# P x V on 32 x 64 array tiles: the column halves take the two heads of a pair instead of two blocks of keys, and ScalarE alone empties the banks

## The chip, the cores and the metric

The kernel runs on one core of one Trainium2 chip. The metric is the device time of one execution in microseconds (us), lower is better. The engines are named as the profile names them: PE is TensorE's matmul side and PEld its weight load, DVE is VectorE, ACT is ScalarE, POOL is GpSimd, and SP issues the transfers.

## The reference

A "macaron" block on x of 2 sequences of 1024 tokens, width 1024, all in fp32: half a feed-forward layer, causal attention with low-rank queries and a shared low-rank latent for keys and values (32 heads, 16 pairs), and half the same feed-forward layer again. Cut to the attention's core:

```python
q = (rmsnorm(x @ wq_a.T) * w) @ wq_b.T            # 32 heads of 64 + 64 (rotary)
kv = rmsnorm(ckv) @ wkv_b.T                       # k_nope 64, v 128 per head, from one latent of 64
scores = einsum('bqhd,bkhd->bhqk', q_full, k_full) * softmax_scale
attn = softmax(where(causal, scores, min))
out = einsum('bqhk,bkhd->bqhd', attn, v).reshape(B, S, H * VD) @ wo.T
```

The kernel multiplies the probabilities by the 64-wide latent itself ("val"), since v is a linear function of it, and folds the value weights into wo.

## The kernel before

The program has phases: a feed-forward phase (f1), a phase for the latents, the attention phase, the output product that starts inside it, and a second feed-forward phase (f2). The change touches the attention phase alone.

**The steps.** Attention works through 32 steps: 16 pairs of heads, and for each pair the two sequences. A step's scores are 16 tiles: 8 rows of 128 queries (t) for each of the two heads (e); tile n is t = n // 2, e = n % 2, and because of causality its width is (t + 1) x 128 keys, at least 256 on TensorE. A prefix and shift name each job in the order tables at L895 to L903: "S8-1" is the job S for tile 8 of the step before.

- S (PE, `scores`): three fp32r products per piece into one of two 1024-wide score buffers in psS.
- M (DVE, L1408): adds the mask, takes the row maximum, and copies the tile to one of 8 `prob` buffers. The score buffer is free when M is done.
- E (ACT, L1357): the exponential in place, with the row sum.
- T (DVE, L1418): transposes each 32 x 32 block of a prob tile into pT. pT exists once; T for row t waits until P x V of the step before has read that row's part (`valued`).
- V (PE, `values`, L1294): P x V, below. V0 waits for T15 of its step.
- Q, F, W (PE): queries of the next step (six products of 512 columns each), the folded query weights (in every other step), and the folded output weights. They write the same four psV banks as V.
- ACT copies each Q out in three instructions (L626 to L628), and POOL rotates it (job A: L633, L635, L637); H (ACT, L644) and B (POOL, L648) split it into a high and a low part. S0 and S1 of a step wait for B0 and B1, S8 and S9 for B2 and B3.
- R (DVE, L1427, L1431) takes the reciprocal of the row sums; SP takes them through DRAM and back as `o_scale` (job X, L1206 and L1210), and P (POOL, L1481) multiplies the value tile `o_raw` by them; Y stores it (L1216).

Each engine runs its jobs strictly in the order of its own table; the tables are written out by hand or by a planner, and the waits are semaphores. In one turn of TensorE's table come S8 to S15 of the step before with Q, F and W among them, then S0 to S7 of this step, then V0 to V7 of the step before.

**P x V.** DVE transposes only within 32 x 32 blocks, so a row group of the array (32 rows) holds 32 keys of four different query blocks i, and each row group i writes its own psV bank i. For each key tile kt (V0 to V7) there are four blocks of 32 keys. Each product has 32 rows and 64 stationary columns (val of one block), and moves both heads at once: 2 x (8 - kt) x 32 columns. Blocks 0 and 1 go to output partitions 0 to 63, blocks 2 and 3 to partitions 64 to 127: 16 products for a key tile. In the trace each of them is two loads and two matmuls. So each bank holds two halves of a sum, which have to be added: ACT copies the upper half (64 x 512) to the unused upper rows of cosT or sinT (`evict_values`, L1366 to L1372; `upper`, L1171), and DVE adds it to the lower half in two instructions, one for each head (`join_values`, L1433 to L1443), and writes o_raw. The profile calls o_raw, o_scale and the query buffers "pT", since they lie in its unused columns.

**The end.** In the last turn DVE splits the first 8 output weights before its four joins, and the other 8 after them; the output product (`tensor_steps`, L1088 in the trace) runs its first pairs meanwhile.

Of the kernel before, what the change touches and what calls it, by code (L numbers as in the profile page):

```python
# [8 lines left out]
ALU = mybir.AluOpType  # L9
ACT = mybir.ActivationFunctionType  # L10
# [6 lines left out]
P = 128  # L17
BANK = 512
# [5 lines left out]
PAIRS = H // 2  # L24
NOPE, ROPE, VD = 64, 64, 128
QHD = NOPE + ROPE
KVR = 64
# [7 lines left out]
QT = S // P  # L35
# [52 lines left out]
def later(n, least):  # L88

    return not isinstance(n, int) or n >= least  # L90
# [104 lines left out]
SLOTS = 4  # L195
# [455 lines left out]
def latents_phase(nc, k, src_d, args, ahead, v_d):  # L651
# [6 lines left out]
    with ExitStack() as stack:  # L658
# [179 lines left out]
        def _(dve):  # L838
# [53 lines left out]
TILES = 2 * QT  # L892
RING = 8
BLOCKS = P // 32
PE_STEP = ("S8-1 F0-1 S9-1 F1-1 Q0+0 S10-1 S11-1 Q1+0 S12-1 S13-1 W0-1 S14-1 S15-1 Q2+0 Q3+0 S0+0 S1+0 S2+0 S3+0 S4+0 "  # L895
           "S5+0 S6+0 S7+0 V0-1 V1-1 V2-1 V3-1 V4-1 V5-1 V6-1 V7-1")
ACT_STEP = ("F0-1 F1-1 E8-1 Q0+0 E9-1 E10-1 Q1+0 E11-1 W0-1 H0+0 E12-1 E13-1 H1+0 E14-1 E15-1 Q2+0 Q3+0 E0+0 E1+0 E2+0 "
            "E3+0 E4+0 E5+0 E6+0 H2+0 E7+0 H3+0 O0-1 O1-1 O2-1 O3-1")
DVE_STEP = ("M15-1 T12-1 T13-1 M0+0 T14-1 M1+0 M2+0 M3+0 T15-1 M4+0 M5+0 T0+0 R1-1 T1+0 T2+0 M6+0 T3+0 M7+0 T4+0 T5+0 "
            "T6+0 R0+0 T7+0 O0-1 M8+0 O1-1 F0+0 M9+0 O2-1 T8+0 F1+0 M10+0 M11+0 T9+0 O3-1 M12+0 M13+0 T10+0 T11+0 "  # L900
            "M14+0")
POOL_STEP = ("B2+0 B3+0 A0+1 A1+1 B0+1 B1+1 P0-1 P1-1 A2+1 A3+1")
SP_STEP = ("X1-1 Y0-1 Y1-1 K0+0 L0+0 X0+0 Z0+0")  # L903


# [201 lines left out]
def attention_phase(nc, k, args, oT_d, rinv_d, wvo_d, v_d, src_d, dst_d):  # L1107
# [6 lines left out]
    with ExitStack() as stack:  # L1114
        c = Ctx(nc, stack)
        queries, cosT, sinT, wn_in, tab_in = k.queries, k.cosT, k.sinT, k.wn_in, k.tab_in
# [6 lines left out]
        pT = c.sb("pT", [P, 2, QT, S])  # L1123
        val = c.sb("val", [P, B, BLOCKS, QT, KVR])
# [5 lines left out]
        psV = c.ps("psV", [P, 4, BANK])  # L1130
# [1 line left out]
        scored, maxed, allowed, exped, turned = c.sem("scored"), c.sem("maxed"), c.sem("allowed"), c.sem("exped"), c.sem("p_turned")  # L1132
        zeroed, recip, r_turned = c.sem("zeroed"), c.sem("recip"), c.sem("r_turned")
        r_stored, r_loaded = c.sem("r_stored"), [c.sem(f"r_loaded{ch}") for ch in range(2)]
        valued, copied, evicted, scaled = c.sem("valued"), c.sem("copied"), c.sem("evicted"), c.sem("scaled")
        o_stored = [c.sem(f"o_stored{ch}") for ch in range(2)]
        w_done, w_copied, w_stored = c.sem("w_done"), c.sem("w_copied"), c.sem("w_stored")
        output = Output(nc, c, {**k.homes, **c.homes}, psS, src_d, dst_d, oT_d, wvo_d, k.early, k.eps_ln)
        units = 2 * PAIRS
        block = stack.enter_context(nc.Block())  # L1140

        def spare(e, t0, t1):

            return pT[:, e, t0:t1, CHUNK:S]

        qf, swapped = spare(0, 0, 2), spare(0, 2, 4)
        o_raw, o_scale = spare(1, 0, 2), spare(1, 2, 4)
# [19 lines left out]
        def folds(it, n, s):  # L1167

            return 2 * (it + (s + 1) // 2) + n + 1

        def upper(bank):  # L1171

            return (cosT, sinT)[bank // 2][0:KVR, bank % 2 * BANK:(bank % 2 + 1) * BANK]

        def by_block(tile, i):

            return tile.rearrange("p h (t a r) -> p h t a r", a=BLOCKS, r=32)[:, :, :, i, :]
# [81 lines left out]
        def _(pe):  # L1259
# [34 lines left out]
            def values(it, kt, s):  # L1294

                step, b = it * 2 + s, s % 2
                if kt == 0:
                    pe.wait_ge(turned, step * TILES + TILES)
                    if not later(step, 2):
                        pe.wait_ge(v_in[step], 16 * BLOCKS * BLOCKS)  # L1300
                for a in range(BLOCKS // 2):
                    for half in range(2):
                        for i in range(BLOCKS):
                            rows, block = slice(32 * i, 32 * i + 32), BLOCKS // 2 * half + a
                            x = kt * P + 32 * block
                            out = psV[KVR * half:KVR * half + KVR, i, :].rearrange("p (e t r) -> p e t r", e=2, r=32)
                            ins = nc.tensor.matmul(out[:, :, kt:QT, :], val[rows, b, block, kt, :], pT[rows, :, kt:QT, x:x + 32],  # L1307
                                                   start=(kt == 0 and a == 0), stop=(kt == QT - 1 and a == BLOCKS // 2 - 1))
                ins.then_inc(valued, 1)

            def fold_output(it, s):
# [8 lines left out]
            def body(r):  # L1320
                for (job, n, s), users in r.bank_users(PE_STEP):
                    vacated(r.it, users)
# [17 lines left out]
        def _(act):  # L1340
# [25 lines left out]
            def evict_values(it, bank, s):  # L1366

                step = it * 2 + s
                act.wait_ge(valued, step * QT + QT)
                if later(step, 1):  # L1370
                    act.wait_ge(evicted, step * 4 + bank - 3)
                nc.scalar.activation(upper(bank), psV[KVR:P, bank, :], ACT.Copy).then_inc(copied, 1)  # L1372

            def body(r):
                for job, n, s in r.jobs(ACT_STEP):
                    if job == "E":
# [24 lines left out]
        def _(dve):  # L1401
# [28 lines left out]
                    dve.wait_ge(r_stored, number * 64 - 192)  # L1430
                nc.vector.transpose(rinvT[:, x // QT, :], rinv[:]).then_inc(r_turned, 1)  # L1431

            def join_values(it, bank, s):  # L1433

                step = it * 2 + s
                dve.wait_ge(copied, step * 4 + bank + 1)
                if later(step, 1):
                    for ch in range(2):
                        dve.wait_ge(o_stored[ch], step * 16)
                for e in range(2):  # L1440
                    x = slice(e * 32 * QT, (e + 1) * 32 * QT)
                    halves = [y.rearrange("p (h t r) -> p h t r", h=2, r=32) for y in (psV[0:KVR, bank, x], upper(bank)[:, x])]
                    ins = nc.vector.tensor_tensor(by_block(o_raw, bank)[KVR * e:KVR * e + KVR], halves[0], halves[1], ALU.add)  # L1443
                ins.then_inc(evicted, 1)

            nc.vector.memset(rinv[:], 1.0).then_inc(zeroed, 1)
            dve.wait_ge(zeroed, 1)

            def body(r):
                for job, n, s in r.jobs(DVE_STEP):  # L1450
                    if job == "M":
                        maxima(r.it, n, s)
                    elif job == "T":
                        transposes(r.it, n, s)
                    elif job == "R":
                        row_scales(r.it, n, s)
                    elif job == "O":
                        if r.last and s == 1 and n == 0:
                            output.weights_lo(nc, dve, range(2 * SLOTS))
                        join_values(r.it, n, s)  # L1460
                    elif job == "F":
                        queries.split_fold_lo(nc, dve, psV[:, n, :], n, folds(r.it, n, s))
            rounds(dve, body)
            output.weights_lo(nc, dve, range(2 * SLOTS, PAIRS))
            output.vector_steps(nc, dve)

        @block.gpsimd
        def _(pool):
# [20 lines left out]
            def body(r):  # L1489
                job, n, s = list(Round(0).jobs(POOL_STEP))[-1]  # L1490
                before = None if r.first else (job, n, s - 2)
                for job, n, s in r.jobs(POOL_STEP):
                    if before:
# [122 lines left out]
```

## Time and profile before

| | |
|---|---|
| time, median of 3 runs | 1892.49 us (1891.0 to 1895.84) |
| span of the profiled execution | 1895.1 us |
| granted TensorE clock, mean over the span | 0.985 |
| DMA | 182.7 MB, 96 GB/s |
| attention steps | 32, one every 29.55 us and 30.96 us in turn |

The profile is of one execution and was taken on the core itself. Its views used below: the page's shares and 40 slices (a digit is the busy share of a slice in tenths); busy time by stretches; the waits, which say for an engine and a line which other line ended its idle time; groups of instructions by line and form with the mean duration of one; and the timeline, in which equal neighbours are merged ("x256") and the time covers all of them. A matmul's duration holds the way through the array, so that durations of neighbours overlap: the pace is read from starts.

### The profile page before, as it was taken

Reading aid. Unit: us, or ns where it says so; the run is one execution under the profiler, and the core shown is the slowest. Engines: PE = TensorE matmul, PEld = TensorE weight load, DVE = VectorE, ACT = ScalarE, POOL = GpSimd, SP = SyncE. Lnnn points to the kernel's source line nnn. Section 1 sums busy time; section 2 is a strip of 40 time slices with the busy share of each in tenths; the row PEclk is TensorE's granted clock in tenths of the full one; section 3 lists DMA queues with packets and bytes.
Section 4 is the critical chain, followed back from the end, with each engine's and each line's share of the span. In section 5 each row is a group of like instructions: output and inputs, shape, how many; then the busy total and the mean of one; then the engine's idle time right before and its main releaser. Section 6 shows DMA issues by size and latency. Waiting matters only on the chain. (4 is left out here: it accounts for less than half of the span.)

```text
span 1895.1 us, 44298 instructions
## 1 busy us (share of the span) xinstructions
PE 1803.7 (95%) x15472; PEld 1422.9 (75%) x15472; DVE 1231.4 (65%) x2654; ACT 1000.5 (53%) x2137; POOL 877.8 (46%) x641
## 2 busy tenths in 40 slices
PE   5999969899999999999999999998999999989999
PEld 4788869877777777777777777775788888877887
DVE  5655358688898888889888888989521111125453
ACT  2221047788887888888787888877310100112110
POOL 3232112377777878777787878775000000014321
PEclk9999979999999999999999999999999999989999
DMA  6542162311212112121222212123742233224321
GB/s 217 193 156 100 67 173 94 84 62 44 86 59 78 57 62 80 57 80 40 85 69 68 69 51 82 55 86 113 249 151 89 94 100 115 67 87 158 130 89 59
DMA packets 111969, 182.74 MB, mean 96 GB/s; under 512 B 27680, under 2 KB 64672, under 8 KB 109856
## 3 DMA queue, kind: packets, MB, share of 16 engines
q1 hardware_dynamic: 111904, 181.88, 29.8%
q8 instruction: 41, 0.67, 0.2%
q14 instruction: 24, 0.20, 0.0%
HBM read 122.33 MB, written 59.51 MB: 96 GB/s over the span
## 5 line engine op out<-in xcount | busy, mean ns | idle before, releaser
L1290 PE MATMUL psS<-keyT,q 128*128 128x512 f32 (+2 forms) x2304 | 473.2, 350 | 23.9 <-POOL q L648 14.5
L1290 PEld LDWEIGHTS psS<-keyT,q 128*128 128x128 f32 x2304 | 381.2, 189 | 118.2 <-DVE negmax L1408 41.7
L1357 ACT ACTIVATE prob<-prob,negmax 128x640 f32<-128x640 f32 (+7 forms) x512 | 392.0, 767 | 78.5 <-DVE negmax L1408 75.9
L1418 DVE STREAM_TRANSPOSE pT<-prob 128x640 f32<-128x640 f32 (+7 forms) x512 | 379.9, 762 | 66.4 <-PE psV L1307 61.6
L1408 DVE CUSTOM_DVE_ANT_0 prob<-psS,mask 128x640 f32<-128x640 f32 (+7 forms) x512 | 371.9, 742 | 20.9 <-PE psS L1290 7.4
L469 PE MATMUL f_psy<-f_weff,f_xT 128*128 128x512 f32 x1344 | 315.6, 393 | 0.0
L1101 PE MATMUL psS<-o_w,o_o 128*128 128x512 f32 x1344 | 304.8, 389 | 0.0
L469 PEld LDWEIGHTS f_psy<-f_weff,f_xT 128*128 128x128 f32 x1344 | 250.9, 188 | 55.8
L1101 PEld LDWEIGHTS psS<-o_w,o_o 128*128 128x128 f32 x1344 | 252.3, 188 | 52.4
L1307 PE MATMUL psV<-pT,val 32*64 32x512 f32 (+3 forms) x8192 | 264.8, 407 | 6.4 <-DVE pT L1418 6.2
L1307 PEld LDWEIGHTS psV<-pT,val 32*64 32x64 f32 x8192 | 168.8, 132 | 109.7 <-issue 66.2
L633 POOL TENSOR_TENSOR pT<-pT,cosT 64x512 f32<-64x512 f32 x124 | 159.6, 1287 | 194.4 <-ACT pT L628 180.5
L275 POOL TENSOR_TENSOR f_weff<-f_w_in,f_weff 128x1024 fp32r<-128x1024 f32 x16 | 39.0, 2437 | 397.5 <-ACT f_weff L388 397.5
L618 PE MATMUL psV<-qnT,wq 128*128 128x512 f32 x744 | 186.4, 393 | 0.4 <-issue 0.4
L1074 DVE TENSOR_TENSOR o_y<-psS,o_x_in 128x512 f32<-128x512 f32 x32 | 22.0, 691 | 252.0 <-PE psS L1101 238.4
L351 POOL TENSOR_TENSOR f_xo<-f_xt,f_bias_half 128x1024 f32<-128x1024 f32 x32 | 81.4, 2543 | 216.7 <-DMA x<-f_xo 103.5
L1023 ACT ACTIVATE o_o<-o_in 128x1024 fp32r<-128x1024 f32 x32 | 32.6, 1055 | 257.2 <-PE psS L1101 235.8
L648 POOL TENSOR_TENSOR q<-pT,q 128x512 fp32r<-128x512 f32 x124 | 160.1, 1291 | 10.9 <-POOL pT L637 2.2
L635 POOL TENSOR_TENSOR pT<-pT,sinT 64x512 f32<-64x512 f32 x124 | 160.0, 1290 | 9.7
L637 POOL TENSOR_TENSOR pT<-pT 64x512 f32<-64x512 f32 x124 | 159.5, 1286 | 9.7
L618 PEld LDWEIGHTS psV<-qnT,wq 128*128 128x128 f32 x744 | 135.3, 188 | 27.0 <-issue 0.6
L179 ACT ACTIVATE f_xT<-f_ps_xT 128x512 fp32r<-128x512 f32 x64 | 35.0, 595 | 172.6 <-PE f_ps_xT L170 172.6
(120 smaller groups left out, 1919.1 us busy)
## 6 DMA issues: line engine op xcount, KB each, us to landing
wo<-in_wo SPq DMA_DIRECT2D x16, 1024.0 KB, 6.0
pT<-row_scales SPq DMA_DIRECT2D x128, 128.0 KB, 2.9
oT<-pT SPq DMA_DIRECT2D x64, 256.0 KB, 2.5
o_in<-oT SPq DMA_DIRECT2D x32, 512.0 KB, 5.2
f_xt<-in_x SPq DMA_DIRECT2D x16, 512.0 KB, 4.4
f_w_in<-in_w SPq DMA_DIRECT2D x16, 512.0 KB, 6.7
w_sum<-f_w_in SPq DMA_DIRECT2D x16, 512.0 KB, 5.3
x<-f_xo SPq DMA_DIRECT2D x16, 512.0 KB, 3.0
```

Source lines behind the costliest of these rows:

```text
L469: ins = nc.tensor.matmul(psy[:, j, half, :], f.xT[:, j, a, dt, :], weff[:, b, m, dt, half * BANK:(half + 1) * BANK], start=(i == 0 and dt ...
L618: ins = nc.tensor.matmul(bank, self.wq[:, a, e, t, :], qnT[:, m, t, x:x + CHUNK], start=(i == 0 and t == 0), stop=(i == 2 and t == QRT - 1))
L633: nc.gpsimd.tensor_tensor(plain, plain, cos, ALU.mult).then_inc(self.rope_parts, 1)
L635: nc.gpsimd.tensor_tensor(crossed, crossed, sin, ALU.mult).then_inc(self.rope_parts, 1)
L637: nc.gpsimd.tensor_tensor(plain, plain, crossed, ALU.add).then_inc(self.roped, 1)
L648: nc.gpsimd.tensor_tensor(self.rows(LO, n), qf, self.rows(HI, n).bitcast(F32), ALU.subtract).then_inc(self.q_lo, 1)
L1101: ins = nc.tensor.matmul(self.ps[:, j, x], self.o[j][:, a, pair, :], self.w[pair][:, m, x], start=(pair == 0 and i == 0), stop=(pair == PA ...
L1290: ins = nc.tensor.matmul(psS[:, slot, start + x0:start + x1], q[:, e, a, t * P:(t + 1) * P], k.keyT[:, m, b * S + x0:b * S + x1], start=(i ...
L1307: ins = nc.tensor.matmul(out[:, :, kt:QT, :], val[rows, b, block, kt, :], pT[rows, :, kt:QT, x:x + 32], start=(kt == 0 and a == 0), stop=( ...
L1357: nc.scalar.activation(row, row, ACT.Exp, bias=negmax[:, n % 8:n % 8 + 1], scale=-1.0, accum_out=rowsum[:, column(n, s):column(n, s) + 1]) ...
L1408: nc.vector.tensor_tensor_reduce(out=prob[:, n % RING, 0:width], in0=place(n), in1=k.mask[:, S - width:S], scale=-1.0, scalar=LARGEST, op0 ...
L1418: nc.vector.transpose(pT[:, n % 2, t, 0:width], prob[:, n % RING, 0:width]).then_inc(turned, 1)
```

## The change

In `values`, a product now takes one head e and one block of 32 keys. The head decides which 64-column half of the array and which 64 output partitions it uses; the four blocks of a key tile accumulate in the same place. So there are 32 products for a key tile instead of 16, each moving (8 - kt) x 32 columns instead of twice that, and val of a block is loaded once for each head. A finished bank holds 128 partitions (two heads x 64) by 256 columns of complete sums. ACT copies it to o_raw in one instruction of 128 x 256 (`evict_values`), and waits itself for the store of the step before to be done with o_raw. The joins on DVE, the semaphore `copied` and the helper `upper` are gone. In the last turn DVE splits all 16 output weights after its table.

The order tables of PE, ACT, DVE and POOL are new, SP's is not. PE: F1 ahead of S9, and W behind S14. ACT: the copy of bank 3 (O3) moves into the next turn, behind F0; W behind H0; E14 ahead of H1; Q2 ahead of E15. DVE: M and T in another order, without joins, R1 directly behind T15, T0 and T1 ahead of M4 and M5. POOL: the two scalings P0 and P1 move from behind B1 to directly behind B3, ahead of A0.

```diff
-PE_STEP = ("S8-1 F0-1 S9-1 F1-1 Q0+0 S10-1 S11-1 Q1+0 S12-1 S13-1 W0-1 S14-1 S15-1 Q2+0 Q3+0 S0+0 S1+0 S2+0 S3+0 S4+0 "
+PE_STEP = ("S8-1 F0-1 F1-1 S9-1 Q0+0 S10-1 S11-1 Q1+0 S12-1 S13-1 S14-1 W0-1 S15-1 Q2+0 Q3+0 S0+0 S1+0 S2+0 S3+0 S4+0 "
            "S5+0 S6+0 S7+0 V0-1 V1-1 V2-1 V3-1 V4-1 V5-1 V6-1 V7-1")
-ACT_STEP = ("F0-1 F1-1 E8-1 Q0+0 E9-1 E10-1 Q1+0 E11-1 W0-1 H0+0 E12-1 E13-1 H1+0 E14-1 E15-1 Q2+0 Q3+0 E0+0 E1+0 E2+0 "
-            "E3+0 E4+0 E5+0 E6+0 H2+0 E7+0 H3+0 O0-1 O1-1 O2-1 O3-1")
-DVE_STEP = ("M15-1 T12-1 T13-1 M0+0 T14-1 M1+0 M2+0 M3+0 T15-1 M4+0 M5+0 T0+0 R1-1 T1+0 T2+0 M6+0 T3+0 M7+0 T4+0 T5+0 "
-            "T6+0 R0+0 T7+0 O0-1 M8+0 O1-1 F0+0 M9+0 O2-1 T8+0 F1+0 M10+0 M11+0 T9+0 O3-1 M12+0 M13+0 T10+0 T11+0 "
-            "M14+0")
-POOL_STEP = ("B2+0 B3+0 A0+1 A1+1 B0+1 B1+1 P0-1 P1-1 A2+1 A3+1")
+ACT_STEP = ("F0-1 O3-2 F1-1 E8-1 Q0+0 E9-1 E10-1 Q1+0 E11-1 E12-1 E13-1 H0+0 W0-1 E14-1 H1+0 Q2+0 E15-1 Q3+0 H2+0 E0+0 "
+            "E1+0 E2+0 E3+0 E4+0 E5+0 E6+0 E7+0 H3+0 O0-1 O1-1 O2-1")
+DVE_STEP = ("T12-1 T13-1 M15-1 T14-1 M0+0 M1+0 M2+0 M3+0 T15-1 R1-1 T0+0 T1+0 M4+0 M5+0 T2+0 M6+0 M7+0 T3+0 T4+0 T5+0 "
+            "T6+0 M8+0 F0+0 R0+0 T7+0 M9+0 F1+0 T8+0 M10+0 M11+0 T9+0 T10+0 M12+0 M13+0 T11+0 M14+0")
+POOL_STEP = ("B2+0 B3+0 P0-1 P1-1 A0+1 A1+1 B0+1 B1+1 A2+1 A3+1")
...
-                for a in range(BLOCKS // 2):
-                    for half in range(2):
+                for block in range(BLOCKS):
+                    for e in range(2):
                         for i in range(BLOCKS):
-                            rows, block = slice(32 * i, 32 * i + 32), BLOCKS // 2 * half + a
-                            x = kt * P + 32 * block
-                            out = psV[KVR * half:KVR * half + KVR, i, :].rearrange("p (e t r) -> p e t r", e=2, r=32)
-                            ins = nc.tensor.matmul(out[:, :, kt:QT, :], val[rows, b, block, kt, :], pT[rows, :, kt:QT, x:x + 32],
-                                                   start=(kt == 0 and a == 0), stop=(kt == QT - 1 and a == BLOCKS // 2 - 1))
+                            rows, x = slice(32 * i, 32 * i + 32), kt * P + 32 * block
+                            out = of_block(psV[KVR * e:KVR * e + KVR, i, :])
+                            ins = nc.tensor.matmul(out[:, kt:QT, :], val[rows, b, block, kt, :], pT[rows, e, kt:QT, x:x + 32],
+                                                   start=(kt == 0 and block == 0), stop=(kt == QT - 1 and block == BLOCKS - 1))
...
                 if later(step, 1):
-                    act.wait_ge(evicted, step * 4 + bank - 3)
-                nc.scalar.activation(upper(bank), psV[KVR:P, bank, :], ACT.Copy).then_inc(copied, 1)
+                    for ch in range(2):
+                        act.wait_ge(o_stored[ch], step * 16)
+                nc.scalar.activation(by_block(o_raw, bank), of_block(psV[:, bank, :]).rearrange("p (h t) r -> p h t r", h=2),
+                                     ACT.Copy).then_inc(evicted, 1)
...
-                for e in range(2):
-                    x = slice(e * 32 * QT, (e + 1) * 32 * QT)
-                    halves = [y.rearrange("p (h t r) -> p h t r", h=2, r=32) for y in (psV[0:KVR, bank, x], upper(bank)[:, x])]
-                    ins = nc.vector.tensor_tensor(by_block(o_raw, bank)[KVR * e:KVR * e + KVR], halves[0], halves[1], ALU.add)
-                ins.then_inc(evicted, 1)
...
-                        if r.last and s == 1 and n == 0:
-                            output.weights_lo(nc, dve, range(2 * SLOTS))
-                        join_values(r.it, n, s)
...
-            output.weights_lo(nc, dve, range(2 * SLOTS, PAIRS))
+            output.weights_lo(nc, dve, range(PAIRS))
```

`of_block(bank)` is the first 256 columns of a bank, seen as 8 rows t of 32.

## Rows read from the trace of the kernel before

**Rows 1.** The page: busy us, share of the span and instructions by engine

```profile
PE 1803.7 (95%) x15472; PEld 1422.9 (75%) x15472; DVE 1231.4 (65%) x2654; ACT 1000.5 (53%) x2137; POOL 877.8 (46%) x641
```

**Rows 2.** Busy us by stretches, from one V start to the next; then clock

```profile
871.09:902.04 30.95, 30.17 (x366) 22.60 (x365) 26.88 (x65) 25.44 (x58) 23.34 (x19) 1.00 0.16 54
902.04:931.59 29.55, 28.78 (x357) 21.52 (x356) 25.94 (x61) 24.65 (x55) 23.05 (x19) 1.00 0.23 80
```

**Rows 3.** Waits of PE and PEld, 500 to 1250 us: total, times, longest

```profile
PE psS L1290 <- POOL q L648: 12.3, 37, 0.4
...
PEld psS L1290 <- DVE negmax L1408: 29.5, 49, 0.8
PEld psS L1290 <- POOL q L648: 13.2, 37, 0.6
...
PEld psV L1307 <- DVE pT L1418: 9.1, 25, 0.4
```

**Rows 4.** Timeline of one V: start, us covered, instructions; then its end alone

```profile
902.04 8.21 PE L1307 MATMUL psV<-pT,val 32*64 32x512 f32 x256
...
909.41 0.84 PE L1307 MATMUL psV<-pT,val 32*64 32x128 f32 x48
...
909.30 0.81 PEld L1307 LDWEIGHTS psV<-pT,val 32*64 32x64 f32 x48
```

**Rows 5.** L1307 alone by key tile, kt = 0, 5, 6 and 7: stretch, us

```profile
902.03:903.80 1.77, 1.76 (x32) 0.77 (x40) 1.00 0.74 168
...
908.53:909.18 0.65, 0.65 (x40) 0.64 (x32) 1.00 0.00 0
909.18:909.63 0.46, 0.46 (x48) 0.46 (x36) 1.00 0.00 0
909.63:910.20 0.56, 0.56 (x48) 0.47 (x34) 1.00 0.02 7
```

**Rows 6.** Groups by form, whole span: busy us, mean ns; idle before

```profile
L1307 PEld LDWEIGHTS psV<-pT,val 32*64 32x64 f32 x8192 | 168.8, 132 | 109.7 <-issue 66.2 <-DVE pT L1418 10.2 <-ACT pT L628 0.6
...
L1443 DVE TENSOR_TENSOR pT<-psV,cosT 64x256 f32<-64x256 f32 x128 | 53.2, 416 | 26.4 <-ACT cosT L1372 25.5
...
L1372 ACT ACTIVATE cosT<-psV 64x512 f32<-64x512 f32 x64 | 34.6, 590 | 19.4 <-PE psV L1307 19.4
...
L777 ACT ACTIVATE qnT<-ps 128x256 fp32r<-128x256 f32 x16 | 6.1, 382 | 1.4 <-PE ps L821 1.4
```

**Rows 7.** Timeline from the end of that V to the next V

```profile
910.64 1.12 PE L1290 MATMUL psS<-keyT,q 128*128 128x384 f32 x6 [0.39 <-POOL q L648]
...
913.94 1.17 SPq L1210 DMA_DIRECT2D pT<-row_scales  x2
...
914.63 0.60 ACT L626 ACTIVATE pT<-psV 128x512 f32<-128x512 f32 x1 [0.78 <-PE psV L618]
...
924.86 2.69 POOL L648 TENSOR_TENSOR q<-pT,q 128x512 fp32r<-128x512 f32 x2
...
926.48 1.14 ACT L1357 ACTIVATE prob<-prob,negmax 128x1024 f32<-128x1024 f32 x1
...
926.97 4.70 PE L1290 MATMUL psS<-keyT,q 128*128 128x256 f32 x24
...
927.81 2.67 POOL L1481 TENSOR_TENSOR pT<-pT 128x512 f32<-128x512 f32 x2 [0.26 <-POOL q L648]
...
930.03 1.24 DVE L1418 STREAM_TRANSPOSE pT<-prob 128x1024 f32<-128x1024 f32 x1
...
931.59 8.21 PE L1307 MATMUL psV<-pT,val 32*64 32x512 f32 x256
```

**Rows 8.** Timeline behind the last V: ACT's copies, DVE's joins, PE's wait

```profile
1339.41 1.08 ACT L1372 ACTIVATE cosT<-psV 64x512 f32<-64x512 f32 x2
...
1342.31 1.73 DVE L1443 TENSOR_TENSOR pT<-psV,sinT 64x256 f32<-64x256 f32 x4
...
1347.64 35.52 PE L1088 MATMUL psS<-o_w,o_o 128*128 128x512 f32 x144 [4.35 <-DVE o_w L1054]
```

More of the change, by code:

```diff
@@ L1134, in attention_phase @@
         r_stored, r_loaded = c.sem("r_stored"), [c.sem(f"r_loaded{ch}") for ch in range(2)]
-        valued, copied, evicted, scaled = c.sem("valued"), c.sem("copied"), c.sem("evicted"), c.sem("scaled")
+        valued, evicted, scaled = c.sem("valued"), c.sem("evicted"), c.sem("scaled")
         o_stored = [c.sem(f"o_stored{ch}") for ch in range(2)]
@@ L1169, in folds, with of_block @@
             return 2 * (it + (s + 1) // 2) + n + 1
-        def upper(bank):
-            return (cosT, sinT)[bank // 2][0:KVR, bank % 2 * BANK:(bank % 2 + 1) * BANK]
+        def of_block(bank):
+            return bank[:, 0:32 * QT].rearrange("p (t r) -> p t r", r=32)
         def by_block(tile, i):
@@ L1431, in row_scales @@
                 nc.vector.transpose(rinvT[:, x // QT, :], rinv[:]).then_inc(r_turned, 1)
[L1433 to L1439, printed above, removed]
-                for e in range(2):
-                    x = slice(e * 32 * QT, (e + 1) * 32 * QT)
-                    halves = [y.rearrange("p (h t r) -> p h t r", h=2, r=32) for y in (psV[0:KVR, bank, x], upper(bank)[:, x])]
-                    ins = nc.vector.tensor_tensor(by_block(o_raw, bank)[KVR * e:KVR * e + KVR], halves[0], halves[1], ALU.add)
-                ins.then_inc(evicted, 1)
             nc.vector.memset(rinv[:], 1.0).then_inc(zeroed, 1)
@@ L1456, in body @@
                         row_scales(r.it, n, s)
-                    elif job == "O":
-                        if r.last and s == 1 and n == 0:
-                            output.weights_lo(nc, dve, range(2 * SLOTS))
-                        join_values(r.it, n, s)
                     elif job == "F":
```

## The prediction

> **What bounds the kernel now.** I read the busy shares first, then the stretches between V starts, then the waits, then the timeline. PE is busy for 95% of the span and DVE for 65% [rows 1], so over the whole program only PE can be the bound. In attention that is less clear: in a step of 29.55 us PE is busy for 28.78, DVE for 25.94, ACT for 24.65 and POOL for 23.05 [rows 2]. The reader is to see four engines that are all nearly full and run fixed orders: a step is a loop of waits rather than one busy engine. PE's waits from 500 to 1250 us (25 steps) are small: DVE's maxima 29.5 us, POOL's split queries 13.2 and 12.3 (largely the same stalls, seen by the load and the matmul), the last transpose before V 9.1 [rows 3], some 2 us a step. So the change can win back 2 us of PE's time a step at most, and all else that it gives DVE is worth nothing.
>
> I cut a step in two: **V itself**, 8.21 us, and **the way from V's end to the next V's start**. One V runs from 902.04 to 910.25 and the next starts at 931.59 [rows 4, 7], so the way is 21.34 us; in a step with the two folds it is 30.95 - 8.21 = 22.74 [rows 2].
>
> **V: twice as many products, each half as long.** The moved columns stay the same, so where a product is bound by its columns nothing changes: two products of 256 for one of 512. It changes where the columns are so few that the instruction is the bound. The key tiles take 1.77 us (kt 0), 0.65 (kt 5), 0.46 (kt 6) and, with what is left of 8.21, about 0.4 (kt 7) [rows 5]. Per matmul of 32 that is 55, 20, 14 and 13 ns, for 512, 192, 128 and 64 columns: it falls with the columns down to 128 and then no longer. The floor, from V's end: 48 matmuls cover 0.84 us, less the last one's own 0.25, over 47 steps: 12.6 ns; 48 loads cover 0.81, less 0.13: 14.5 ns [rows 4]. I take 13.5 ns. After, a key tile has 64 matmuls and never takes under 64 x 13.5 = 0.86 us. Kt 4 (128 columns then) is at it already. Added: kt 5 0.86 - 0.65 = 0.21, kt 6 0.86 - 0.46 = 0.40, kt 7 0.86 - 0.40 = 0.46, and some 0.05 of seams in the other five: **+1.1 us a step**. Low end: 12.6 ns, +0.9. High end: a load takes 132 ns [rows 6], and if eight are under way at a time and no more, 16.5 ns each, 1.06 us a key tile: kt 4 +0.19, kt 5 +0.41, kt 6 +0.60, kt 7 +0.66, +1.9 us a step. The trace has short products only at V's end, behind a full queue; whether the pace holds for 256 of them it doesn't show. I stay near the rows measured back to back.
>
> The trace thus shows 13 ns for a matmul of 64 columns [rows 4]. The Trainium skill, TensorEngine Tiling, section Performance Considerations (Instruction Overhead), speaks against this change: each matmul has some 60 cycles of overhead, and one should not tile a dimension that is already small. Taken as 25 ns an instruction at 2.4 GHz, an estimate from that page, V would last at least 512 x 25 ns = 12.8 us instead of the 9.3 that the rows give. By that rule 256 instructions now would need 6.4 us, which 8.21 allows, but its last 48 would need 1.2 us and take 0.84, so the trace disagrees.
>
> **V's end to the next V.** *ACT.* Four copies of 64 x 512 at 590 ns become four of 128 x 256, for which a row of the same size reads 382 ns [rows 6]; the new output pattern is not in the trace, so 0.38 to 0.6. The new waits on `o_stored` cost nothing while the outputs are stored 20 us before. Behind the copies stands E8, and behind that the copy of Q0, which needs PE's S8, S9 and Q0 anyway: S8 takes 1.12 us for 6 matmuls now with its neighbour gap, clean about 0.87. Clean, S8 and S9 end at 1.74 us after V and Q0 at 3.1, and ACT's Q0 copy starts at 3.4; even at 0.6 each the copies end at 2.4 and E8 (0.93) at 3.3. *DVE.* Eight additions of 416 ns go [rows 6], 3.3 us a step, and with them M8 to M13 are no longer queued behind the joins. *PE.* S8 waited 0.39 us for POOL [rows 7] and S9 again; POOL gets P (2.67 us for two, now between B1 and A2 [rows 7]) out of the way, and Q2 is copied before E15, so B2 and B3 are ready by V's end. Now the Q0 copy starts at 914.63, 4.38 after V's end; after at 3.4.
>
> From there the loop goes through ACT's queue. From the Q0 copy to E15 (914.63 to 926.48) ACT does Q0, E9, E10, Q1, E11, W, H0, E12, E13, H1, E14 in 11.85 us, of which about 0.45 is waiting [rows 7]; the new order has the same set up to H1, so H1 ends at 3.4 + 11.4 = 14.8, with 0.1 to 0.3 for new waits 15.0. Then POOL's B1, 1.3 us, ends at 16.4 and S1 starts at 16.6; now B1 ends at 924.86 + 2.69 = 927.55, which is 17.3. S1 to S7 need 3.45 clean (PE's 927.3 to 931.4 is 4.1 with DVE's stalls). The next V starts at 20.0 instead of 21.34. T15 is next latest: H1 15.0, Q2 1.8, E15 1.15, T15 1.24 [rows 7] and 0.3 to V make 19.5, so it is hidden with 0.5 to spare. In fold steps the order adds 1.25 (two folds 1.1 and their ACT copies) instead of 1.4. **Won back: 1.3 and 1.5, 1.4 us a step.** Bounds: nothing, if one of the moved jobs comes late; 2.0 if PE ran free.
>
> *POOL and SP.* P now stands ahead of A0, which must start at 5.2 (Q0 copied). P needs all four copies (1.9 after V, 2.9 in a fold step) and its scales. Those loads are issued at 913.94 now, 3.7 after V's end [rows 7], and would be late there: P would end at 10.4. But they sit there because SP first had to issue the stores of a P that ran at 927.81. With P early SP is free; its K waits for W's copy at 13.4, the first scale job follows with the 8 us it takes now, the second starts at about 22 and has landed by 29, just at V's end (20.0 + 9.3). R1, now straight after T15, is ready long before. So P runs 2 to 5 us after V, and A0 is not held; the margin is 2 us.
>
> **The end.** Behind the last V DVE's joins end at 1344.0 and PE waits 4.35 us, to 1347.6, for the ninth output weight [rows 8]. Without joins DVE starts 1.7 us earlier, ACT's copies are 0.4 shorter: PE goes on at about 1345.5, **-2.1**, and the last V's own growth is hidden by this wait.
>
> **Sum.** 31 x (1.1 - 1.4) = -9.3, end -2.1: -11.4 on the profiled 1895.1 gives 1883.7; the median lies 2.6 below the profiled span, so **1881 us**. The term that carries it is a difference of two like numbers, each uncertain by half a microsecond a step, or 15 us.
>
> **The rivals.**
> - *Slower: the short products run at 16.5 ns.* Place: kt 4 to 7 of every V. Price: +1.9 for +1.1, 31 x 0.8 = +25: 1906. It decides the sign from 13.5 + 1.5 ns on (0.36 us a step over some 224 matmuls). For it: loads alone come in stretches of 14.5 ns; against: the 12.6 of matmuls. Chance 0.25. Beyond it, the same mechanism with kt 5's 20 ns as the least that a long train of short products keeps: kt 3 to 7 then take 1.28 us each, +3.0 a step for +1.1, +59: 1940, chance 0.02. The Trainium skill's rule above points this way; with its 25 ns it would be 3.5 us a step and 1989, an estimate from that page.
> - *Slower: P holds A0.* If scales or copies land late, every us moves A0, A1, B0, B1, S1 and V; it eats the gain from 1.4 on. With P at 7.5 instead of 5.2: +2.3 in the 16 steps that have K, +37, or half of that: 1900 to 1918. Chance 0.13.
> - *Faster: PE runs free.* If B1 is no limit (H1 earlier than I queue it), V follows at 19.3: 0.7 x 31 = -22: 1859. Chance 0.15.
> - *It doesn't do what it says*: the copies cost 0.6 or more. Hidden by Q0, as above; no time of its own.
>
> Forecast 0.42, own range 1871 to 1894; the rest 0.03. The range 1859 to 1912 leaves out 0.2. Faster means below 1886.8, slower above 1898.2, since 0.3% is about what a measurement can tell from none. Forecast case: 0.30 faster, 0.11 same, 0.01 slower; free PE 0.14 faster, 0.01 same; short products 0.05 same, 0.22 slower; P late 0.02 faster, 0.03 same, 0.08 slower; the rest slower. Together 0.46, 0.20, 0.34.
>
> **What would show it.** V: 9.3 us from start to end, kt 5 to 7 each about 0.86. The way: S8 within 0.2 us of V's end; Q0's copy at 3.4; S1 at 16.6 behind POOL's B1, V at 20.0. Periods 29.3 and 30.5. P at 2 to 5 after V. Wrong: V over 9.7 (the pace), A0 behind P, or DVE's maxima still among PE's waits.

## The result: 13% slower, and the profile after

The changed kernel takes **2150.49 us** (median of 4, 2139.67 to 2153.14) where the kernel before takes 1893.61 (median of 4, 1891.0 to 1895.84) in the same comparison: a ratio of **1.1345**, 95% interval 1.1316 to 1.1375. The forecast was 1881 with a range of 1859 to 1912. The profiled execution spans 2150.4 us, 255 more than before's.

The busy shares come first, as in [rows 1], and two more lines of the page below them: the granted clock in 40 slices, and one DMA queue.

```profile
PE 1909.2 (89%) x23664; PEld 1595.6 (74%) x23664; DVE 1149.9 (53%) x2398; ACT 976.7 (45%) x2137; POOL 875.1 (41%) x641
...
PEclk9999899989989899889888989989889999999999
...
q8 instruction: 209, 3.42, 0.7%
```

DVE has lost its 256 joins (82 us), ACT 24 us, and PE has 8192 more matmuls, as the diff says. PE's busy share *fell*, from 95% to 89%: it stands still for longer. The clock is at 8 tenths in many slices where before's was at 9 in nearly all. And the queue q8, which carries instructions and was 41 packets and 0.67 MB before, carries 209 packets and 3.42 MB. The page of before, for comparison:

```profile
PEclk9999979999999999999999999999999999989999
...
q8 instruction: 41, 0.67, 0.2%
```

What PE waits for over the whole span (line, releaser, us in total, times, longest):

```profile
PE psV L1305 <- issue: 109.1, 78, 4.2
PE psS L1289 <- issue: 57.7, 13, 4.7
```

"Issue" means that no semaphore, engine or transfer that the profile knows holds the engine back. In attention before, PE's matmuls have two such waits, of 0.4 and 0.2 us; there they wait as in [rows 3], and the 12.3 us for POOL is no longer among PE's longer waits. L1305 is the product P x V, L1289 the score product, of which the first behind a V is meant.

One V in the timeline, to be laid beside [rows 4] (start, us covered, instructions, in brackets the idle time before):

```profile
811.12 3.81 PE L1305 MATMUL psV<-pT,val 32*64 32x256 f32 x142
815.44 2.64 PE L1305 MATMUL psV<-pT,val 32*64 32x192 f32 x128 [0.51 <-issue]
819.19 1.95 PE L1305 MATMUL psV<-pT,val 32*64 32x128 f32 x128 [1.11 <-issue]
822.93 1.50 PE L1305 MATMUL psV<-pT,val 32*64 32x64 f32 x114 [1.79 <-issue]
```

The pieces behind the first are 128 matmuls long, with as many loads, whatever the columns. A key tile has 64 matmuls, so two of them are as long; but the first stop comes after 142 matmuls (14 into the third key tile), and in the next V after 284 (28 into the fifth). So it is neither a key tile's data nor a bank that PE waits for. And in this V, the shorter the products, the longer the stop. The next V ends like this; the loop's back branch stands behind it:

```profile
857.19 1.35 PE L1305 MATMUL psV<-pT,val 32*64 32x64 f32 x100 [2.11 <-issue]
862.74 1.97 PE L1289 MATMUL psS<-keyT,q 128*128 128x384 f32 x6 [4.20 <-issue]
```

Stretches over one turn of PE's loop (two steps), with the columns of [rows 2]: V, the first scores, the rest of the way, then V again and the whole way behind it.

```profile
811.12:824.45 13.33, 9.92 (x514) 8.86 (x513) 5.27 (x16) 5.73 (x18) 7.19 (x6) 0.99 0.19 64
824.45:829.30 4.85, 4.85 (x20) 4.55 (x21) 2.61 (x8) 2.14 (x6) 2.58 (x2) 0.68 0.14 54
...
846.08:858.54 12.46, 9.62 (x513) 8.83 (x512) 5.06 (x16) 5.73 (x18) 7.21 (x6) 0.99 0.08 27
858.54:888.86 30.32, 25.36 (x109) 20.50 (x108) 19.14 (x41) 19.04 (x39) 16.02 (x13) 0.78 0.16 56
```

V takes 13.3 and 12.5 us for 8.21, of which PE is busy for under 10, and behind it the granted clock is 0.68 and 0.78. The DMA view of the same turn counts, beside the data on q1, this:

```profile
q8 instruction: 12, 0.20, 1.1%
```

Twelve blocks of 16 KB (0.20 MB) are fetched in one turn. In a turn of before (811.12 to 871.09) the same view has q1 alone. The stops in V lie 256 PE instructions apart (or a multiple of it), and 16 KB over 256 is 64 bytes an instruction: the stops lie at the seams of the fetched blocks. The transfers fit too. In the whole trace after, V has 70 stops of over 0.5 us; 69 of them end 2.2 to 3.0 us after the start of a transfer on q8, and the last one is a wait for DVE's transpose.

**The account.** From the first V's start to the last one's end the kernel before takes 945 us, the changed one 1208: all of the loss, and 8 us more. Idle times of over 0.65 us between PE's matmuls sum to 7 us in before (2 of them) and 170 in after (85): +162. The clock is at its lower level, 1.2 GHz, for 7 us there before and for 234 after; in the turn shown it falls at V's end, behind stops of 0.5, 1.1 and 1.8 us and again behind 0.7 and 2.1. PE is busy for 176 of the 234 us. The first six score products behind a V take 1.97 us at the lower level and, in e2 below, half of 2.05 at the upper one, so about half of the 176 is lost, 88 us (an estimate). In the turn shown, 77.7 us for 60.5 in [rows 2], the stops of V and of the back branch sum to 10.5 (0.5, 1.1, 1.8, then 0.7, 2.1 and 4.2) and another behind them is 0.6. The clock takes 1.6 behind the first V (4.85 x 0.32) and 4.3 behind the second (half of the 8.6 us that PE is busy at 0.50). That is 17.0 for a loss of 17.2. What the short products add and what the order gives are not in it; by the runs below they nearly cancel out.

### The profile page after: what moved, and what is told of

Same layout as the page of the kernel before. It is cut to its first block and busy times, and to the rows that moved or that the text cites. A ratio compares the mean times of both kernels' runs of the same rounds, so it can differ in the third digit from the quotient of the medians.

```text
span 2150.4 us, 60219 instructions
## 1 busy us (share of the span) xinstructions
PE 1909.2 (89%) x23664; PEld 1595.6 (74%) x23664; DVE 1149.9 (53%) x2398; ACT 976.7 (45%) x2137; POOL 875.1 (41%) x641
## 3 DMA queue, kind: packets, MB, share of 16 engines
q8 instruction: 209, 3.42, 0.7%
## 5 line engine op out<-in xcount | busy, mean ns | idle before, releaser
L1408 DVE CUSTOM_DVE_ANT_0 prob<-psS,mask 128x640 f32<-128x640 f32 (+7 forms) x512 | 377.6, 749 | 362.6 <-PE psS L1289 344.8
L1289 PE MATMUL psS<-keyT,q 128*128 128x512 f32 (+2 forms) x2304 | 502.5, 371 | 65.7 <-issue 57.7
L1289 PEld LDWEIGHTS psS<-keyT,q 128*128 128x128 f32 x2304 | 415.2, 208 | 150.5 <-issue 86.9
L1305 PE MATMUL psV<-pT,val 32*64 32x256 f32 (+2 forms) x16384 | 316.9, 297 | 113.9 <-issue 109.1
L1305 PEld LDWEIGHTS psV<-pT,val 32*64 32x64 f32 x16384 | 285.9, 134 | 153.0 <-issue 132.0
L1464 POOL TENSOR_TENSOR pT<-pT 128x512 f32<-128x512 f32 x64 | 82.2, 1285 | 350.2 <-ACT pT L1371 340.2
L618 PE MATMUL psV<-qnT,wq 128*128 128x512 f32 x744 | 204.8, 421 | 2.2 <-issue 2.2
L618 PEld LDWEIGHTS psV<-qnT,wq 128*128 128x128 f32 x744 | 149.2, 208 | 32.8 <-issue 2.9
```

The lines of the kernel that those rows point to most:

```text
L618: ins = nc.tensor.matmul(bank, self.wq[:, a, e, t, :], qnT[:, m, t, x:x + CHUNK], start=(i == 0 and t == 0), stop=(i == 2 and t == QRT - 1))
L1289: ins = nc.tensor.matmul(psS[:, slot, start + x0:start + x1], q[:, e, a, t * P:(t + 1) * P], k.keyT[:, m, b * S + x0:b * S + x1], start=(i ...
L1305: ins = nc.tensor.matmul(out[:, kt:QT, :], val[rows, b, block, kt, :], pT[rows, e, kt:QT, x:x + 32], start=(kt == 0 and block == 0), stop= ...
L1408: nc.vector.tensor_tensor_reduce(out=prob[:, n % RING, 0:width], in0=place(n), in1=k.mask[:, S - width:S], scale=-1.0, scalar=LARGEST, op0 ...
```

## The experiments

My theory after the profile: **PE's loop body no longer stays where PE reads its instructions from, so it is fetched anew in each turn, and in V, where the instructions are shortest, PE is through a block before the next has arrived.** The rivals: the array's halves taken by heads, or the new order, cost the time by themselves (e1, e2); it is short products at V's end, not their number (e3, e4); it is not the number of instructions but the kind of product (e11 with e10 as its control, e13). All edits are in P x V, in the tables, or in the passes.

**Every product split, everything else as before (e1).** Banks, joins and tables are those of before; each product runs once per head.

```diff
-                    for half in range(2):
+                    for heads in (slice(0, 1), slice(1, 2)):
+                      for half in range(2):
...
-  nc.tensor.matmul(out[:, :, kt:QT, :], val[rows, b, block, kt, :], pT[rows, :, kt:QT, x:x + 32],
+  nc.tensor.matmul(out[:, heads, kt:QT, :], val[rows, b, block, kt, :], pT[rows, heads, kt:QT, x:x + 32],
```

> The kernel before with one thing changed: in all eight key tiles each product is split by head, so there are as many PE instructions as after the change (16384 matmuls of P x V) while the tables, the joins on DVE and the layout of the sums stay. Fetch theory (PE's loop body no longer stays in its instruction store, so it is fetched again every turn and P x V runs out of instructions): the instruction queue moves some 3.4 MB instead of 0.67, the stretch of one V is 12 to 14 us with gaps of 1 to 2.5 us every second key tile, and the time is 2120 to 2170 us. Rival, the new order tables or ACT's wait for o_stored: they are not in this kernel, so it stays at the pace of short products alone, 1893 + 32 x 1.1 = 1928 us, with 0.67 MB of instructions.

2215.31 us, ratio 1.1688 (1.1666 to 1.1709): more than the changed kernel and more than expected. Of the 65 us between the two, e2 below gives 36 to the joins and the order that e1 keeps. On its page, the instruction queue:

```profile
q8 instruction: 209, 3.42, 0.7%
```

And PE's waits, whole span:

```profile
PE psV L1308 <- issue: 145.8, 88, 4.5
PE psS L1290 <- issue: 55.9, 13, 4.5
```

The number of products alone brings the loss, twelve fetches a turn with it. The heads' place in the array, the tables and ACT's wait for `o_stored` are cleared. Another 29 us between e1 and the changed kernel are not explained; e1's V is longer, 12 to 17 us.

**The new order without the split (e2).** The changed kernel with before's 16 products a key tile. The joins are left out and ACT's copies take the first 256 columns of a bank, so the two halves are never added: less is computed.

```diff
-                for block in range(BLOCKS):
-                    for e in range(2):
+                for a in range(BLOCKS // 2):
+                    for half in range(2):
...
```

> The kernel after with one thing taken back: P x V issues before's 16 products a key tile (both heads in each, the column halves take different blocks). The halves of the sums are not added and ACT copies only the first 256 columns of a bank, so the joins are left out of the computation; copies, waits, tables and DVE's relief are those of after. Fetch theory: 0.67 MB of instructions, V back at 8.2 us, and the order change can show its worth: my prediction's 1.4 us a step and 2.1 at the end give 1893 - 45 = 1848 us. Rival (tables or waits are what costs): still over 2100 us.

1857.6 us, ratio 0.9805 (0.9789 to 0.9822). Its q8 is back at before's 41 packets. The timeline from one V to the next, beside [rows 7]:

```profile
887.07 8.21 PE L1306 MATMUL psV<-pT,val 32*64 32x512 f32 x256
...
895.21 2.05 PE L1289 MATMUL psS<-keyT,q 128*128 128x384 f32 x12
895.31 1.21 ACT L1372 ACTIVATE pT<-psV 128x256 f32<-128x256 f32 x4 [1.54 <-PE psV L1306]
...
896.69 2.67 POOL L1465 TENSOR_TENSOR pT<-pT 128x512 f32<-128x512 f32 x2 [1.51 <-ACT pT L1372]
...
898.73 0.60 ACT L626 ACTIVATE pT<-psV 128x512 f32<-128x512 f32 x1 [0.27 <-PE psV L618]
...
908.94 2.69 POOL L648 TENSOR_TENSOR q<-pT,q 128x512 fp32r<-128x512 f32 x2
...
915.48 6.83 PE L1306 MATMUL psV<-pT,val 32*64 32x512 f32 x163
```

V ends at 895.28. S8 runs straight on, the Q0 copy starts 3.45 us after V's end, POOL's B1 ends 16.35 after it, and the next V starts at 20.20: the way that the prediction worked out (3.4, 16.4, 20.0). So the order gives what it should where nothing is fetched, and without the split there is no loss: the level of 1.2 GHz, too, is granted for 3.4 us in its attention and not for 234.

**The split in a part of the key tiles (e3, e4, e7, e9).** As e1, but only for the key tiles named.

```diff
+  for heads in ([slice(0, 1), slice(1, 2)] if kt in (0, 1, 2) else [slice(0, 2)]):   # e3
+  for heads in ([slice(0, 1), slice(1, 2)] if kt in (5, 6, 7) else [slice(0, 2)]):   # e4
+  for heads in ([slice(0, 1), slice(1, 2)] if kt in (7,) else [slice(0, 2)]):        # e7
+  for heads in ([slice(0, 1), slice(1, 2)] if kt in (6, 7) else [slice(0, 2)]):      # e9
```

> The kernel before with the products of key tiles 0 to 2 alone split by head: 192 more PE instructions in a step, 384 in the loop body (about 1500 to 1890, of 64 bytes: 94 to 118 KB). The columns are 256, 224 and 192 there, so that the stream is the bound. If the instruction store holds 128 KB: no more fetches than before, V at 8.25 us and 1893 to 1897 us. If it holds less than 118 KB: fetches in every turn, and 50 to 150 us more.

> The kernel before with the products of key tiles 5 to 7 alone split by head (96, 64 and 32 columns): the same number of added instructions as e3 (118 KB), but all of them short. It prices short products without the others. My prediction's 13.5 ns each: key tiles at 0.86 us, +1.1 us a step, 1893 + 34 = 1927 us or less where the slack of the step takes some. Rival (short products alone run dry, at 25 ns or more each): +3 us a step and more, above 1975 us.

> The kernel before with key tile 7 alone split by head: 64 more PE instructions in a step, 128 in the loop body (about 1630, 102 KB). Looks for the limit between 94 KB (no fetches) and 118 KB (nine in every turn). If it lies above 102 KB: 0.67 MB, key tile 7 longer by 0.3 to 0.45 us, 1894 + 12 = 1906 us. If below: seven or eight fetches in every turn, over 2.2 MB, and 150 us or more on top.

> The kernel before with key tiles 6 and 7 split by head: a loop body of about 1760 PE instructions, 112 to 113 KB, between e7 (102 KB, none fetched) and e3 (118 KB, nine in every turn). If the limit is in whole blocks of 16 KB and seven of them fit (112 KB), this one lies on it; with fetches: eight or nine a turn, 2.4 MB or more and over 2020 us; without: 0.67 to 0.7 MB and 1900 to 1910 us.

| kernel | matmuls in the body | q8 packets | fetches a turn | us | ratio (95%) |
|---|---|---|---|---|---|
| before | 720 | 41 | 0 | 1893.6 | 1 |
| e7, kt 7 | 784 | 42 | 0 | 1899.74 | 1.0027 (1.0011 to 1.0042) |
| e9, kt 6, 7 | 848 | 98 | 2 and 7 in turn | 1997.98 | 1.0547 (1.0526 to 1.0568) |
| e3, kt 0 to 2 | 912 | 162 | 9 | 2084.57 | 1.1014 (1.0990 to 1.1039) |
| e4, kt 5 to 7 | 912 | 162 | 9 | 2113.78 | 1.1158 (1.1109 to 1.1206) |
| e1, all | 1232 | 209 | 12 | 2215.31 | 1.1688 (1.1666 to 1.1709) |

e3 splits only the longest products, which stay at 192 columns or more (before's key tile 5 has as many in one product) and so were free by every price that the prediction worked out from rows. It costs 10%. e4 was made to price the short products and can't, being fetched as e3 is. The first 64 matmuls more cost 6 us, the next 64 cost 98. That is a step between two sizes of the body and not a price for each product. (For e9 I had expected eight or nine fetches in every turn and over 2020 us.) e3's waits are of after's two kinds:

```profile
PE psV L1308 <- issue: 61.1, 33, 3.6
PE psS L1290 <- issue: 50.3, 13, 4.6
```

**Many instructions with V untouched (e13).** Before, with the three passes of the score and query products issued twice (the sums come out doubled). V's 16 products a key tile stay.

```diff
-                    for i, (a, m) in enumerate(PASSES):
+                    for i, (a, m) in enumerate(PASSES * 2):
```

> The kernel before with each pass of the scores' and the queries' fp32r products issued twice (they are then summed double, so the scores are twice too large): the loop body has 912 matmuls, as many as e3, of which 384 are fp32r and 528 belong to fp32 products as in before. If all PE instructions count alike: nine fetches a turn as in e3, 2.6 MB. If an fp32 product takes more room than an fp32r product beyond its two matmuls (e7 and e11 say so), none: 0.6 to 0.75 MB, V at 8.2 us. PE's own work grows by some 17 us a step either way, so the time is about 2350 to 2450 us.

2538.46 us, above the 2350 to 2450 that I had put on it; most of the growth is the second set of passes. It has 912 matmuls in the body, like e3, and exactly e3's 162 packets, nine a turn. Its V and what follows it:

```profile
1019.56 8.21 PE L1307 MATMUL psV<-pT,val 32*64 32x512 f32 x256
1032.17 3.07 PE L1290 MATMUL psS<-keyT,q 128*128 128x384 f32 x12 [4.40 <-issue]
```

Here V is whole again, at 8.21 us, though the body is fetched: its block of 16 KB lasts longer, and the fetches keep up. The stop at the back branch stays (61.4 us over 13 times). So there are two costs: the back branch, whatever the body holds, and the stops in stretches of short instructions. The odd steps, with the back branch, take 54 to 58 us; the first of them, which is not yet fetched, takes 47.9. That is 6 to 10.5 us a turn, of which 4 to 5 are the stop; the rest fits the clock behind it, which is at its lower level for 3 to 14 us a turn.

**Fewer instructions elsewhere to make room (e10, e11).** Scores and queries with one pass of three (two products are left out), first alone (e10), then with key tiles 0 to 2 split (e11).

```diff
-                    for i, (a, m) in enumerate(PASSES):
+                    for i, (a, m) in enumerate(PASSES[:1]):
```

> The control for e11: the kernel before with one of the three passes of the scores' and the queries' products (the two correction passes are left out), a body of some 1250 PE instructions. No fetches, V at 8.2 us; the steps end up with DVE or ACT as the bound, some 26 to 28 us.

> e3 with the same two correction passes left out as in e10: the split of key tiles 0 to 2 is there in full, but the body has some 1630 PE instructions instead of 1890, as many as e7's. Fetch theory: no fetches, V back from e3's 10 and 13 us to 8.2 to 8.3, time within 0.3% of e10's. Rival (the split products cost by themselves, as weight loads or banks): V stays at 10 us and more, and the time is 60 us or more above e10's.

e10: 1929.11 us, ratio 1.0183 (1.0163 to 1.0204). With less work for PE it is slower: PE waits for the other engines and its mean granted clock falls to 0.87 of 2.4 GHz, from 0.985. Its V takes 9.6 to 11.1 us though nothing is fetched there, so V's length says nothing in e11, and the packets have to decide. e11: 1979.31, ratio 1.0448 (1.0427 to 1.0469), 50 us over e10. I had expected it to be free of fetches, at 784 matmuls in the body like e7. It fetches two and seven blocks in turn, like e9. This is a miss, and it limits the theory: between e7 and e11 the number of matmuls does not decide. Both lie at the edge; where the body stands against the 16 KB blocks may, which I did not vary.

**V with few instructions but short ones (e6).** The changed kernel, with key tiles 1 to 4 reduced to one product each (their part of the result is left out), to see the pace of split products that are not fetched.

```diff
+                            if kt in (1, 2, 3, 4) and (block, e, i) != (3, 1, 3):
+                                continue
```

> The kernel after with most of P x V's key tiles 1 to 4 left out (one product of 32 each instead of 32), so that its body has as many instructions as before's (about 1520) and still holds the short products of key tiles 5 to 7. Fetch theory: 0.67 MB of instructions, no gaps, key tiles 5 to 7 at 0.80 to 0.86 us each (13 ns a matmul), whole time under 1820 us. Rival (short products starve PE by themselves): key tiles 5 to 7 at 1.6 us or more, gaps of a microsecond as in after.

1827.99 us in one run (I had expected under 1820), 41 packets, no stops in V. V without the four key tiles:

```profile
869.97 5.20 PE L1307 MATMUL psV<-pT,val 32*64 32x256 f32 x264
```

From first start to last, key tile 7 takes 0.65 us for 64 matmuls; key tile 6 takes 0.68 to 0.84 from its start to the next one's. Key tile 5 takes 1.09 to 1.16, here right behind the single products; in the changed kernel, where no stop falls into it, 0.80 to 0.84.

**What in the order earns it (e5, e12).** e2 with all of before's tables (e5), and e2 with only POOL's place of P as before (e12, whose edit against e2 stands below).

```diff
-POOL_STEP = ("B2+0 B3+0 P0-1 P1-1 A0+1 A1+1 B0+1 B1+1 A2+1 A3+1")
+POOL_STEP = ("B2+0 B3+0 A0+1 A1+1 B0+1 B1+1 P0-1 P1-1 A2+1 A3+1")
```

> e2 with before's order tables (without the joins in DVE's): the computation leaves out the joins as e2 does. It splits e2's 36 us. If they come from the empty places of the joins in DVE's queue (my prediction: DVE's maxima no longer late), most of it stays: 1858 to 1870. If the new order brings it (P ahead of A0, O3 and W later, R1 earlier), it falls back to 1880 to 1893.

> e2 (wide products, joins left out, after's tables) with before's order on POOL alone: P0 and P1 behind B1 again. My prediction said P ahead of A0 makes room so that B2 and B3 are ready at V's end. If that carries the order's 25 us (e2 against e5): 1875 to 1883. If ACT's order (Q2 ahead of E15, copies first) carries it: 1857 to 1865.

e5: 1882.85, ratio 0.9939 (0.9923 to 0.9956). e12: 1881.23, 0.9928 (0.9912 to 0.9945). Of e2's 36 us the joins' absence, with ACT's shorter copies, is worth 11; the order is worth 25, and nearly all of it hangs on P's place in POOL's queue. PE's waits for POOL from 500 to 1250 us show it, here in e12:

```profile
PE psS L1289 <- POOL q L648: 22.1, 37, 0.7
```

In e2, same stretch, PE's matmuls have no such wait, and of the waits for POOL only the load's is left:

```profile
PEld psS L1289 <- POOL q L648: 4.7, 12, 0.4
```

**The order with the joins kept (e8, e14).** e8: before's products and joins with the changed tables of PE, ACT and DVE (DVE's O jobs put between T6 and T8), POOL's old. e14: before's tables with P ahead of A0, R1 directly behind T15, and the joins drawn closer together behind V. Both compute everything.

```diff
-POOL_STEP = ("B2+0 B3+0 A0+1 A1+1 B0+1 B1+1 P0-1 P1-1 A2+1 A3+1")
+POOL_STEP = ("B2+0 B3+0 P0-1 P1-1 A0+1 A1+1 B0+1 B1+1 A2+1 A3+1")   # e14
...
```

> The kernel before, with its products and its joins on DVE, under after's tables of PE and ACT, and of DVE with the joins put in behind T6, M8, T7 and F1; POOL keeps before's. Full computation. It asks what the order is worth alone and whether there is something to keep. If the order carries part of e2's gain: 1870 to 1885. If the gain is DVE's freed time alone: 1890 to 1900.

> The kernel before, full computation, with two things of the new order: P0 and P1 directly behind B3 on POOL, R1 directly behind T15 on DVE; and the four joins moved together on DVE right behind V (O0, M8, O1, O2, F0, O3, M9) so that P can start. If the order's gain needs no free DVE: 1870 to 1885. If the joins held together delay M9 and with it S11, or P holds A0: 1895 to 1940.

e8: 1960.34, ratio 1.0348 (1.0331 to 1.0365), a miss. e14: 1932.46, 1.0205 (1.0188 to 1.0222). In e14 POOL waits with P, and A0 behind it, for the joins (500 to 1250 us):

```profile
POOL pT L1481 <- DVE pT L1443: 107.8, 23, 5.0
```

In e8 DVE's transposes wait 95.5 us for ACT and ACT's H jobs 75.0 for POOL: three of the new tables don't go with the old fourth. P needs all the joins where they are kept, and what stands behind P needs P out of the way. So neither of these two tries had the order's gain together with the joins, and no kernel that ran here computes everything and is faster than before.

## Why the prediction was wrong

**The step that failed** is the first: "V: twice as many products, each half as long". It priced an added product by its columns and by the pace at which PE executes, and added "some 0.05 of seams in the other five" key tiles. It never asked where 1024 more PE instructions in a loop body (512 matmuls and 512 loads) come from. V takes 12 to 15 us in all but the last two steps, for the forecast 9.3; the stop behind it and the lower clock come on top. None of the rivals was this one: the slowest, 1940, still was a pace. e3 shows it best, a split which was free by all of my prices from rows and costs 191 us.

The page of before held a hint that I read past: q8, the instructions' own queue, 41 packets for the whole program and none in a turn of the loop. The body stayed in place; a change that adds two thirds to it asks whether it still does. The Trainium skill, Runtime: NRT & Kernel Launch, section Instruction fetch mechanics, speaks of it, and I did not weigh it: instructions come in blocks of 16 KiB, 256 instructions each, PE's store holds 128 KiB, or 2048 instructions, and a taken branch to a target outside "the current 2-page window" costs a fetch before work goes on. The blocks agree with the runs (stops 128 matmuls and loads apart), and so does the price of the branch where the body is fetched (3.4 to 5.2 us). The window does not: before's body of some 1500 instructions, six blocks, is branched back over with no packet on q8. If all of the 128 KiB kept a loop's body, which the page does not say, 2048 instructions would stay. Here 1886 (e3 and e13: twice 912, and some 62 others) were fetched in every turn, so the measured limit is lower. It also says that crossing a block is mostly hidden; in e13's long products it is, in V's short ones it costs 0.5 to 2.1 us each time in the turn shown.

Point by point:

- **The pace, 13.5 ns (the term that I thought carried the sum).** Held, if anything too dear. Unfetched, kt 7 takes 0.65, kt 6 0.68 to 0.84 and kt 5 0.80 to 0.84 us for the 0.86 each that I gave; e7's V is 8.50 for 8.21, +0.29 where kt 7 alone had +0.46. The term, by these, is +0.7 to +0.9, its seams of 0.05 counted, and not +1.1 us a step. The rival of 16.5 ns falls, and with it the one of 20 ns. So does, on these tiles, the Trainium skill's rule of 60 cycles a matmul in TensorEngine Tiling (Array Packing), section Performance Considerations: 64 matmuls of 32 columns in 0.65 us are 10 ns each, less than half of the 25 ns estimated from it.
- **The way from V to V.** Right in its mechanism and nearly in its size. e2: 20.20 for 20.0, Q0's copy at 3.45, B1's end at 16.35. The steps with folds won less: e2's period there is 30.25 for 30.96, 0.7 for the 1.5 that I gave. In attention that makes 30 us (945.6 to 915.4) for 43.
- **ACT's copies.** 386 ns each, at the low end of 0.38 to 0.6, and hidden as said. The changed kernel's groups by form (busy us, mean ns; idle before):

```profile
L1371 ACT ACTIVATE pT<-psV 128x256 f32<-128x256 f32 x128 | 40.3, 386 | 201.5 <-PE psV L1305 201.5
```

- **P ahead of A0 does not hold it.** Right: P runs 1.4 to 4.1 us after V in e2. That this place of P is what wins most of the way, I had not seen; I had put the gain on ACT's queue. e12 corrects it.
- **The end.** -2.1 was forecast. In e2 PE's wait before the output products is 1.00 us for the 4.35 of [rows 8], so it was somewhat more; outside of attention e2 is 8 us shorter in all, of which I can't place the rest.

Without the fetches the sum would have stood about where it was put: e2's 1857.6, and on it some 0.75 us a step, 23 us, for the short products, makes about 1880. That is an estimate from e2, e6 and e7. The changed kernel with its whole V and a body that stays was not tried, so this is argued and not shown.

**What is shown and what stays open.** Shown: the fetches come with the size of the body away from the limit, whatever it is filled with (e3, e4, e13 alike at nine a turn); without them neither the split (e7, e6) nor the order (e2) costs more than a few us; the stops lie at the seams of the blocks and at the back branch, and end 2.2 us or more after a transfer on q8 begins. Open: the exact limit, since e7 and e11 with equal counts differ, and why one or two blocks a turn more are fetched than the body's own size asks for (some 118 KB in e3 and nine blocks, 144 KB); a body that doesn't begin at a seam touches one block more, which is argued and not shown. The lower clock goes with the fetches (e2 without them has it for 3.4 us of attention, the changed kernel for 234), but what it costs by itself no run separates.

## What to carry to other kernels

Before adding instructions to a loop body, count the body's instructions on that engine (64 bytes each here) and look at the instruction queue's packets inside one turn: zero means that it stays, and the change has to keep it so. Here it did at some 1500 PE instructions, did in one kernel and not in another at some 1630, and did not from 1760 on. Here a stall that the profile lays to "issue", at equal numbers of instructions and not at equal data, was a fetch. Then fewer instructions helped (e2), and so did longer ones (e13's V has no stop); the new order did not make up for it.

## What the hardware showed that I had not expected

- An overfull body is fetched whole in every turn and not by its excess alone: 720 matmuls give 0 fetches, 912 give 9, 1232 give 12; at 848 turns of 2 and of 7 alternate.
- PE takes 128 short load and matmul pairs (1.9 to 2.6 us of work) and then stands for 0.5 to 2.1 us in the turn shown, 4.2 at most; the block's transfer began 0.3 to 1.9 us before PE ran dry, and PE went on 2.2 to 2.7 us after that beginning.
- Stops are paid twice: in the turn shown the clock is at 1.2 GHz from V's end on (the granted clock is 0.50 from 858.54 to 872.00, then 1.00). PE is busy for 8.6 us of it, so some 4.3 us are lost (an estimate) beside the stop of 4.2.
- On eight tiles of 32 x 64, matmuls of 32 columns start closer together than I knew. The stretch below (us, PE busy and matmuls, PEclk) begins in e6 with key tile 7's first start. Its 87 matmuls are the 64 of that key tile and 23 still under way. PE is busy for 0.87 us; less the last matmul's 0.22, over 63 steps, that is 10 ns, for 12.6 in [rows 4].

```profile
874.30:875.30 1.00, 0.87 (x87) 1.00 0.00 0
```
